# Attention plus FFN on one core: chunk 0 starts on its own rows, shuffled on chip, and the other blocks are prepared inside it

## The reference

```python
qkv = einsum(x, w_qkv); q, k = rope(rmsnorm(q) * q_scale), rope(rmsnorm(k) * k_scale)
out = softmax(q @ k.T * 8 ** -0.5) @ v            # per head, 1024 keys
x = layernorm(x + out @ w_proj + b_proj)
h = silu(x @ w1.T * s1) * (x @ w2.T * s2)         # 128 -> 512
h = gelu(h @ h1.T * sh1); h = gelu(h @ h2.T * sh2)  # 512 -> 512, exact gelu
x = layernorm(x + h @ w3.T * s3)                  # 512 -> 128
```

## Time and profile before

| | us |
|---|---|
| median of 3 runs | 394.11 (391.36 to 394.29) |
| profiled execution: its time | 395.17 |
| its span | 393.5 |
| TensorE busy | 338.4 (86%) |
| ScalarE busy | 306.3 (78%) |
| VectorE busy | 203.4 (52%) |
| GpSimd busy | 18.4 (5%) |

### The profile page before, as it was taken

How to read it: one execution, slowest core, us unless ns; L and a number is a source line. 1 busy time by engine, 2 the same in 40 slices (tenths; PEclk the granted TensorE clock), 3 DMA queues, 4 the chain that set the end, 5 groups by cost and what they waited for, 6 DMA issues and landing times.

```text
span 393.5 us, 6182 instructions
## 1 busy us (share of the span) xinstructions
PE 338.4 (86%) x2077; PEld 136.4 (35%) x2077; DVE 203.4 (52%) x397; ACT 306.3 (78%) x347; POOL 18.4 (5%) x21
## 2 busy tenths in 40 slices
PE   7977287887799998988899989988999899869990
PEld 2533111111133244433322444442223435325760
DVE  1799844311054664455447624554467253556764
ACT  1458289999999988798999889869998987771530
POOL 2400000000010000001100000001100000011001
PEclk9989679999999999999999999989999999898997
DMA  7987953033021230030303300303030200000001
...
DMA packets 16201, 31.33 MB, mean 80 GB/s; under 512 B 1522, under 2 KB 5106, under 8 KB 16178
## 3 DMA queue, kind: packets, MB, share of 16 engines
...
q0 software_dynamic: 240, 0.79, 0.5%
...
## 4 chain that ended last, share of the span: by engine, by line
PE 55%; ACT 20%; DVE 12%; issue 11%; ACTq 0%; DVEq 0%; POOLq 0%; POOL 0%
PE ps L455 17%; ACT probs L714 17%; PE ps L502 14%; PE ps L442 9%; PE ps L576 4%; PE ps L492 4%; DVE ffn L894 2%; DVE probs L801 2%; DVE probs L810 2%; PE ps L628 1%; PE ps L612 1%; PE ps L594 1%; PE ps L415 1%; DVE parts L790 1%; PE ps L472 1%
## 5 line engine op out<-in xcount | busy, mean ns | idle before, releaser
L714 ACT ACTIVATE probs<-ps 128x1024 f32<-128x1024 f32 x256 | 241.3, 1049 | 33.7 <-PE ps L442 33.6
L455 PE MATMUL ps<-probs,va 128*9 128x512 f32 x1024 | 131.0, 601 | 14.1 <-ACT probs L714 12.3
L442 PE MATMUL ps<-qa,ka 32*128 32x512 f32 x512 | 74.3, 501 | 17.8 <-ACT probs L714 11.7
L442 PEld LDWEIGHTS ps<-qa,ka 32*128 32x128 f32 x512 | 29.8, 184 | 115.1 <-ACT probs L714 72.7
L894 DVE TENSOR_SCALAR ffn<-ps,col 128x512 f32<-128x512 f32 x36 | 27.0, 751 | 55.0 <-PE ps L502 50.9
L502 PE MATMUL ps<-g_hi,w_hi 128*128 128x512 f32 x108 | 47.0, 435 | 2.4 <-DVE ffn L894 2.4
L502 PE MATMUL ps<-g_lo,w_hi 128*128 128x512 f32 x108 | 44.1, 409 | 0.0
L455 PEld LDWEIGHTS ps<-probs,va 128*9 128x9 f32 x1024 | 17.8, 89 | 62.6 <-ACT probs L714 32.4
L831 DVE STREAM_TRANSPOSE o_tok<-ps 128x512 f32<-128x512 f32 x15 | 10.7, 715 | 46.0 <-PE ps L455 46.0
L502 PEld LDWEIGHTS ps<-g_hi,w_hi 128*128 128x128 f32 x108 | 21.0, 194 | 15.6 <-DVE ffn L894 4.3
L869 DVE TENSOR_TENSOR g_lo<-ffn,g_hi 128x512 fp32r<-128x512 f32 x36 | 24.9, 692 | 1.2
...
## 6 DMA issues: line engine op xcount, KB each, us to landing
...
va<-v_all SPq DMA_DIRECT2D x16, 144.0 KB, 4.5
...
```

Source lines behind the costliest of these rows:

```text
L442: mm = pe.matmul(s_tile(u)[:, i, :], ka[rows, slot, kt * P:(kt + 1) * P], qa[rows, slot, :], start=True, stop=not shifted)
L455: mm = pe.matmul(ps[32 * h:32 * h + VW, O_BANK, :], va[:, g % 2, kt, h, :], probs[:, step % 4, h, :], start=(kt == 0), stop=(kt == KT - 1))
L714: nc.scalar.activation(probs[:, step % 4, 2 * pair:2 * pair + 2, :], s_tile(u), ACT.Exp).then_inc(exp_done, 1)
```

## The change

- The prologue prepares only what chunk 0's first groups need: k and q of block 0, k of block 1 and V of blocks 0 and 1, each in instructions of 512 columns. Input loads are put on two queues, SP's and ScalarE's.
- Rows of head groups 0 and 1 no longer go through DRAM for chunk 0: `direct_rows` takes them from the prepared tile with a shuffle among 32 partitions, a copy that rounds to the high part, and a scaled sum that writes the rows into `ka` and `qa`. The columns of the weights are permuted on the host so that a group's features lie in each 32 partitions; `strips` reads the DRAM rows in the matching order. V of these groups is read from `v_all`. Groups 2 and 3 and all later chunks still go through DRAM.
- The other q and k (`LATE`: five tiles) and V of blocks 2 and 3 are made inside chunk 0: 18 tasks (`TASKS`) at fixed slots (`TASK_SLOTS`) through bank 7, with squares and inverse roots between ScalarE's exponentials (`SQUARE_STEPS`, `RINV_STEPS`).
- The FFN weights are loaded by GpSimd in three stages into a smaller buffer, and split in pieces among VectorE's late work; the bias is added on VectorE at the end of chunk 0.
- One warm-up of 13 matmuls becomes one of 8; the second, of 10, goes. ScalarE loads the table for the later chunks after chunk 0.
- The form with row maxima (`wide == 1`) is changed to match; it does not run.

```diff
-MIX_FIRST = 1
+MIX_FIRST = 18
...
+WARM = 8
...
+DIRECT = {0: 2, 2: 3, 4: 4, 8: 6, 12: 7}
+LATE = ((1, Q), (2, K), (2, Q), (3, K), (3, Q))
+TASKS = (("proj", 0), ("swap", 0), ("var", 0),
+ ("proj", 1), ("swap", 1), ("var", 1),
+ ("proj", 2), ("swap", 2), ("var", 2), ("v", 2),
+ ("proj", 3), ("swap", 3), ("var", 3),
+ ("proj", 4), ("swap", 4), ("var", 4), ("v", 3), ("flag", 0))
+TASK_SLOTS = (12, 18, 20, 23, 25, 27, 30, 34, 36, 39, 41, 43, 45, 47, 50, 52, 54, 60)
+SQUARE_STEPS = (7, 12, 16, 21, 24)
+RINV_STEPS = (11, 14, 19, 23, 27)
...
+def strips(scr, g):
+    return scr.rearrange("(j r) t -> j r t", j=HG)[:, bass.ds(HD * PARTS * PARTS * g, HD * PARTS * PARTS)]
...
+    sp.dma_start(wq[:, 0:4 * P], w_qkv[:, 0:4 * P]).then_inc(in_w, 16)
+    sp.dma_start(col[:, 0:NCOL], cols).then_inc(in_cols, 16)
+    sp.dma_start(sinT[:, 0:CH], sines[:, 0:CH]).then_inc(in_rope[0], 16)
+    load_x(1)
+    sp.dma_start(wq[:, 4 * P:5 * P], w_qkv[:, 4 * P:5 * P]).then_inc(in_wv, 16)
+    sp.dma_start(sinT[:, CH:SEQ], sines[:, CH:SEQ]).then_inc(in_rope[1], 16)
     for t in range(2, NCH):
-        sp.dma_start(xT[:, t * CH:(t + 1) * CH], x_t[:, t * CH:(t + 1) * CH]).then_inc(in_x[t], 16)
+        load_x(t)
...
+    store(0, 0, 0)
+    store(1, 0, 1)
+    store(2, 1, 0)
...
+        stored_rows((0, 1), (0,))
         load_group(0, 2)
+        store(3, 1, 1)
+        store(4, 2, 0)
         load_group(0, 3)
-        later_loads(False)
+        store(5, 2, 1)
+        store(6, 3, 0)
+        stored_rows((), (1,))
+        load_group(1, 0)
+        store(7, 3, 1)
+        for g in range(1, NG):
+            load_group(1, g)
+        stored_rows((2, 3), (2, 3))
+        sp.wait_ge(v_evac, 4)
...
-    pool.wait_ge(in_res, 64)
-    pool.tensor_tensor(xb[:], xb[:], bias_b[:, None, :].to_broadcast([P, NCH * TILES, P]), ALU.add).then_inc(res_add, 1)
+    def stage(src, at, blocks):
+        pool.dma_start(w_raw[:, at:at + blocks * src.shape[1]].rearrange("p (k o) -> p k o", k=blocks),
+                       src.rearrange("(k p) o -> p k o", p=P)).then_inc(in_ffn, 16)
+    pool.wait_ge(qk_proj, 4)
+    stage(h1, 0, HM)
+    pool.wait_ge(w_taken, 1)
+    stage(h2, 0, HM)
+    pool.wait_ge(w_taken, 2)
+    stage(w1, 0, 1)
+    stage(w2, HID, 1)
+    stage(w3, 2 * HID, HM)
...
+    def first_task(n):
+        kind, i = TASKS[n]
+        bank = mix(0)
+        if n == 0:
+            pe.wait_ge(rot_done, 6)
+        if kind == "flag":
+            pe.wait_ge(w_split, 1)
+            mm = pe.matmul(bank[0:1, 0:1], ve[:, 0:1], ones_c[:], start=True, stop=True)
+        elif kind == "v":
+            mm = project_v(bank, i)
+        elif kind == "var":
+            pe.wait_ge(late_sq, i + 1)
+            mm = variance(bank, late_sets[i % 2][0])
+        else:
+            t, of = LATE[i]
+            pe.wait_ge(in_x[t], 16)
+            mm = proj(of + (QS if kind == "swap" else 0), bank, t)
+        mm.then_inc(mix_ready, 1)
+    def first_chunk(shifted):
+        use[0], given = 0, 0
+        for step in range(STEPS):
+            logits(0, step, 0, shifted)
+            logits(0, step, 1, shifted)
+            if 2 * step in TASK_SLOTS:
+                first_task(TASK_SLOTS.index(2 * step))
+            if step == 1:
+                pe.wait_ge(o_rows_set, 1)
+            if step:
+                values(0, step - 1)
+            if 2 * step + 1 in TASK_SLOTS:
+                first_task(TASK_SLOTS.index(2 * step + 1))
+        assert use[0] == len(TASKS) == MIX_FIRST
...
+    proj(K, ps[:, 0, :], 0).then_inc(qk_proj, 1)
+    proj(KS, ps[:, 1, :], 0).then_inc(qk_proj, 1)
+    pe.wait_ge(in_means, 16)
+    pe.wait_ge(sq_done, 1)
+    variance(ps[:, 4, :], sq_k).then_inc(var_ready, 1)
+    proj(Q, ps[:, 2, :], 0).then_inc(qk_proj, 1)
+    proj(QS, ps[:, 3, :], 0).then_inc(qk_proj, 1)
+    pe.wait_ge(sq_done, 2)
+    variance(ps[:, 5, :], sq_q).then_inc(var_ready, 1)
+    pe.wait_ge(in_x[1], 16)
+    proj(K, ps[:, MIX_BANK, :], 1).then_inc(qk_proj, 1)
+    proj(KS, ps[:, O_BANK, :], 1).then_inc(qk_proj, 1)
+    pe.wait_ge(in_wv, 16)
+    pe.wait_ge(ln_done, 2)
+    project_v(ps[:, 5, :], 0).then_inc(v_proj, 1)
+    pe.wait_ge(sq_done, 3)
+    variance(ps[:, 4, :], sq_k1).then_inc(var_ready, 1)
+    pe.wait_ge(rot_done, 2)
+    project_v(ps[:, 0, :], 1).then_inc(v_proj, 1)
     pe.wait_ge(bound_flag, 1)
     wide = pe.value_load(flags_i[0:1, 0:1], min_val=0, max_val=1)
-    pe.wait_ge(rot_done, 4 * NCH)
-    pe.wait_ge(ln_done, NCH)
-    for _ in range(WARM_AGAIN):
-        pe.matmul(ps[:, 4, :], warm[:, 0:P], warm[:], start=True, stop=True)
-    pe.wait_ge(v_evac, NCH)
-    pe.wait_ge(in_res, 64)
+    pe.wait_ge(rot_done, 4)
+    pe.wait_ge(v_evac, 2)
+    pe.wait_ge(ln_done, 3)
...
+    act.dma_start(xT[:, 0:CH], x_t[:, 0:CH]).then_inc(in_x[0], 16)
+    act.dma_start(cosT[:, 0:CH], cosines[:, 0:CH]).then_inc(in_rope[0], 16)
+    act.dma_start(mean8[:], means).then_inc(in_means, 16)
+    act.dma_start(srow[:], scale_rows).then_inc(in_scales, 16)
+    act.dma_start(cosT[:, CH:SEQ], cosines[:, CH:SEQ]).then_inc(in_rope[1], 16)
...
+    def inverse_root(n, bank, dst):
+        act.wait_ge(var_ready, n)
+        nc.scalar.activation(dst, bank, ACT.Ln, bias=eps_c[:]).then_inc(ln_done, 1)
+        act.wait_ge(ln_done, n)
+        nc.scalar.activation(dst, dst, ACT.Exp, scale=-0.5).then_inc(rinv_done, 1)
...
+    act.wait_ge(qk_proj, 1)
+    square(ps[:, 0, :], sq_k)
+    inverse_root(1, ps[:, 4, :], rinv_k)
+    act.wait_ge(qk_proj, 3)
+    square(ps[:, 2, :], sq_q)
+    inverse_root(2, ps[:, 5, :], rinv_q)
+    act.wait_ge(qk_proj, 5)
+    square(ps[:, MIX_BANK, :], sq_k1)
+    take_v(1, ps[:, 5, :])
+    inverse_root(3, ps[:, 4, :], rinv_k1)
+    take_v(2, ps[:, 0, :])
...
+    def late_square(n):
+        act.wait_ge(mix_ready, TASKS.index(("proj", n)) + 1)
+        if n >= 2:
+            act.wait_ge(parts_done, PARTS * (n + 2))
+        nc.scalar.activation(late_sets[n % 2][0], ps[:, MIX_BANK, :], ACT.Square).then_inc(late_sq, 1)
+    def late_inverse_root(n):
+        at = TASKS.index(("var", n))
+        dst = late_sets[n % 2][0]
+        act.wait_ge(mix_ready, at + 1)
+        nc.scalar.activation(dst, ps[:, MIX_BANK, :], ACT.Ln, bias=eps_c[:]).then_inc(mix_free, 1)
+        act.wait_ge(mix_free, at + 1)
+        nc.scalar.activation(dst, dst, ACT.Exp, scale=-0.5).then_inc(rinv_done, 1)
...
+        if step in SQUARE_STEPS:
+            late_square(SQUARE_STEPS.index(step))
+        if step in RINV_STEPS:
+            late_inverse_root(RINV_STEPS.index(step))
+    act.preload_act_table_set("exp_and_others")
...
+    def turned_by(bank, of, t, dst):
+        table, at = ((cosT, (C_Q, C_K)), (sinT, (C_QS, C_KS)))[of >= QS]
         half = (t % 2) * CH
-        dve.wait_ge(sq_done, t + 1)
-        wait(dve, h_done, t)
-        for i, c_, table, dst in ((0, C_Q, cosT, rot_a), (1, C_K, cosT, rot_a), (2, C_QS, sinT, rot_b), (3, C_KS, sinT, rot_b)):
-            if i == 2:
-                if t:
-                    low_part(t - 1)
-                dve.wait_ge(qk_proj, 2 * t + 2)
-            nc.vector.scalar_tensor_tensor(
-                out=dst[:, (i % 2) * CH:(i % 2 + 1) * CH], in0=ps[:, i, :], scalar=col[:, c_:c_ + 1],
-                in1=table[:, half:half + CH], op0=ALU.mult, op1=ALU.mult).then_inc(rot_done, 1)
-        dve.wait_ge(rot_done, 4 * t + 4)
-        link(nc.vector.tensor_tensor(rot_a, rot_a, rot_b, ALU.add), 0)
-        if t == NCH - 1:
-            dve.wait_ge(v_evac, t)
-            nc.vector.memset(ps[:, O_BANK, :], 0.0).then_inc(o_rows_set, 1)
-        dve.wait_ge(rinv_done, t + 1)
-        nc.vector.tensor_tensor(hn, rot_a, rinv, ALU.mult).then_inc(h_done, 1)
-    dve.wait_ge(h_done, NCH)
-    last = parts_of(NCH - 1)
-    nc.vector.tensor_copy(last[:, 0, :], hn).then_inc(last_parts, 1)
-    dve.wait_ge(last_parts, 1)
-    nc.vector.tensor_tensor(last[:, 1, :], hn, last[:, 0, :].bitcast(F32), ALU.subtract).then_inc(last_parts, 1)
+        return nc.vector.scalar_tensor_tensor(out=dst, in0=bank, scalar=col[:, at[of % 2]:at[of % 2] + 1],
+                                              in1=table[:, half:half + CH], op0=ALU.mult, op1=ALU.mult)
+    def rope_of(count, h, rot, rinv, n):
+        dve.wait_ge(rot_done, count)
+        link(nc.vector.tensor_tensor(h, h, rot, ALU.add), 0)
+        dve.wait_ge(rinv_done, n)
+        link(nc.vector.tensor_tensor(h, h, rinv, ALU.mult), 0)
...
+    def direct_rows(h, lo, n, g, low, dst):
+        src = spread[:, 0:n]
+        wait(dve, direct, written[0])
+        written[0] += 1
+        link(nc.vector.stream_shuffle(src, h[:, lo:lo + n], [HD * g + m // 4 for m in range(32)]), 0)
+        link(nc.vector.tensor_copy(x_hi[:, 0:n], src), 0)
+        nc.vector.scalar_tensor_tensor(out=dst, in0=x_hi[:, 0:n].bitcast(F32), scalar=col[:, low:low + 1], in1=src,
+                                       op0=ALU.mult, op1=ALU.add).then_inc(direct, 1)
...
+    def rows_parts(n, t, at, h):
+        if t >= 2:
```

(157 more changed lines are left out.)

309 lines of the change are left out of this document (132 added, 177 removed).

## The result

Measured side by side, the kernel after takes 411.88 us (409.33 to 414.11, 4 runs) against 394.12 (391.36 to 394.29): ratio 1.0468, 95% interval 1.0424 to 1.0513. The change makes the kernel slower by 17.8 us. The forecast was 404.6, 390 to 411: right in direction, 7.3 us too low, and 0.9 us outside its range.

What follows compares the result with a forecast made beforehand. The prologue and ScalarE's exponentials in chunk 0 were taken to bound the kernel. Prologue -24.0, chunk 0 +33.9 and boundary +0.6 gave +10.5 us: 405.7 against the profiled execution, 404.6 against the median, range 390 to 411.

Steps and rivals of the forecast that it cites:

- first exponential: End of the prologue: ScalarE's first exponential of chunk 0 comes at 23.4 us instead of 47.36, a gain of 24.0.
- ScalarE's own work in chunk 0: Chunk 0: 58.9 us of exponentials plus 9.0 of squares, logarithms, small exponentials and hand-over, 67.9 us.
- entry of chunk 0 at low clock: Start of chunk 0: TensorE, slow after its gap, adds 1.1 us, as before the change.
- S: Chunk 0: stalls since all 18 tasks share one bank and ScalarE and TensorE are strictly in order, 20.1 us.
- F: Chunk 0: falls of TensorE's clock after idle gaps, three taken at 4.8 us, bounds 0 and six falls, 9.6.
- boundary: Before chunk 1: ScalarE's table load of 1.28 us, beside the 0.69 it waits there now, adds 0.6 us.
- steps 13 and 22: Chunk 0: two swap tasks in the same step as the square releasing their bank's reader, 2.45 us idle each.
- six falls in chunk 0 alone: Chunk 0: rival with six clock falls, 409 us; chance 0.15 together with VectorE being late.
- The fetch: Before the first logits: TensorE's jump over the unused form of chunk 0 stalls for instructions again, 6.1 us.
- Hidden hand-overs: Chunk 0: rival with next logits already in PSUM when ScalarE comes back, net -10.4, 383.7 us; chance 0.13.
- the border S + F = 14.4: Chunk 0: stalls plus clock falls below 14.4 us make the change faster, with the fetch counted.
- VectorE's lateness: Chunk 0: rival with late rows of group 1 or late V, 3 to 5 us more; chance 0.15 with more falls.

Runs made afterwards that it cites:

- a_fill: The kernel after, with 3 to 10 matmuls on zeros on TensorE before ten of the 18 tasks, while it would wait: 404.38 us, ratio 1.0238.
- the two exchanges: TensorE's form for wide == 0 put before the one for wide == 1: in the kernel after 407.61 us, in the kernel before 386.92 us.
- a_resched: The kernel after, with squares, inverse roots and tasks at other steps and VectorE's list in matching order, same work: 384.04 us, ratio 0.973.

## Why the direction was right and the size was not

The change point by point, all in the profiled executions, where the forecast was 405.7 and the time 409.33: 3.6 us off.

| | forecast | after | off |
|---|---|---|---|
| first exponential | 23.4 | 22.34 | -1.1 |
| ScalarE's own work in chunk 0 | 67.9 | 69.5 | +1.6 |
| entry of chunk 0 at low clock | 1.1 | 1.5 | +0.4 |
| stalls and falls, S + F | 20.1 + 4.8 | 25.9 | +1.0 |
| chunk 0 | 93.9 | 96.9 | +3.0 |
| boundary | +0.6 | +0.6 | 0 |
| later chunks and tail | 0 | +1.7 | +1.7 |

Chunk 0 is 22.34 to 119.24; 25.9 is the 32.1 us of waits less 4.7 before the first exponential and 1.5 at steps 2 and 3 (0.97 + 0.56); the own work is what is left.

**The stalls were right one by one.** `a_fill` gives them at full clock. Its 26.3 us of waits less 4.5 at the start and 1.5 at steps 2 and 3 (1.10 + 0.42) are 20.3; the forecast's S was 20.1. By place, forecast and `a_fill`: steps 13 and 22, 2.45 and 2.50 each; steps 18 and 26, 1.6 and 1.72; step 28, 2.0 and 2.00; steps 12, 20 and 24, 1.0 and 0.98 to 1.02; step 10, 1.7 and 2.00; step 21, 1.7 and 1.46. Chains built from single rows of before (read, product, wake, projection, logits) hold to 0.1 us where no VectorE queue is in them.

**The mis-sized term is the clock, F.** It was set to three falls in chunk 0, 4.8 us, and to none elsewhere. The profiled execution had four falls behind the entry, 25.9 - 20.3 = 5.6. The forecast counted them by the length of TensorE's gaps, and the length does not decide alone. Of TensorE's nine idle stretches over 1.3 us in chunk 0 of after, behind its entry, those of 1.38, 2.39, 2.39 and 1.79 us had a fall behind them, and three of 1.63, one of 1.78 and the longest, 2.61, had none. TensorE's lines behind the shortest of the nine (the clock is 0.50 from 44 to 46 us) and the longest (1.00 from 109 to 113):

```profile
42.69 1.78 PE L447 MATMUL ps<-xT,wq 128*128 128x512 f32 x2 [1.38 <-DVE ffn L899]
...
109.20 1.16 PE L451 MATMUL ps<-wq,xT 128*128 128x128 f32 x8 [2.61 <-ACT ffn L812]
```

The profiled execution also had a longer fall in chunk 1, and this lies outside the forecast's sum: ScalarE waits 4.38 us at the place where before waited 1.33, and one less of 1.6 in chunk 2 (1.33 where before had 2.94). That makes +1.4 of the +1.7. ScalarE's timeline of after, chunks 1 and 2:

```profile
196.99 3.77 ACT L822 ACTIVATE probs<-ps 128x1024 f32<-128x1024 f32 x4 [4.38 <-PE ps L478]
...
276.93 3.77 ACT L822 ACTIVATE probs<-ps 128x1024 f32<-128x1024 f32 x4 [1.33 <-PE ps L478]
```

The other 3.6 us are the medians': the profiled execution of after is the fastest of its four, 2.5 below the median, and that of before 1.1 above its own. The forecast knew the second and could not know the first. So the profiled execution alone would lie inside the range of 390 to 411, and the median misses it by 0.9. Executions of after differ in how long TensorE is at low clock: the mean granted clock is 0.946, 0.943, 0.942 and 0.939 for 409.33, 411.66, 412.09 and 414.11 us. With the idle stretches filled the spread falls to 0.5 us at 0.965 to 0.967. So a change that leaves TensorE waiting at many places pays for the falls and for their chance as well, and the range's upper end, six falls in chunk 0 alone, was too near. That the kernel with fills is 7.5 us faster is shown, although its profiled prologue was 1.95 us slower. So at the medians the falls may cost 9 us and not 4.8, an estimate that takes all its executions to have had that slow prologue. How the chance of a fall divides over the places is not shown.

**ScalarE's own work** was short by 1.6. One exponential alone takes 1.02 us, two in a row 1.94, four 3.77: 0.92 each, and 0.1 more at the end of the row. The sum had 0.92 for all, and after breaks the row 18 times with a wait, which by this estimate is 1.8 us.

**The fetch.** Mechanism right, size not: 6.1 was taken, and 3.9 were seen, 2.2 less. Against that the V copies ended 1.0 later than worked out (17.62, not 16.6) and the step from logits to exponential took 0.2 more, so the forecast start is only 1.1 too late, and luck hides half of the error. Where the form stands first the gap is gone in both kernels. The queue's line for 16 to 22 us of after shows one 16 KB transfer, where the gap of before has two:

```profile
q8 instruction: 1, 0.02, 1.3%
```

The DMA queues moved 351 GB/s in the gap of before (40.4 to 46.4 us) and 4 in that of after (17.6 to 21.6). Whether the number of transfers or this traffic makes the gap of before longer is open. The Trainium skill ("Runtime: NRT & Kernel Launch", section "Instruction fetch mechanics") says that a taken branch to a target that is not held waits until its page is fetched. The transfers in both gaps and the two exchanges agree with it; a size for it only the runs give.

**The rivals.** Hidden hand-overs were priced at 383.7 with S about 4 and F 0. The change doesn't do this, but `a_resched` does, at 384.04 with 3.8 us of waits behind the first exponential: the border S + F = 14.4 was the right thing to watch, and one order of the same work lies on each side of it. That the two times are so close is in part luck: S is 2.5 and not 4 (without steps 2 and 3) and the start is 1.1 sooner, but ScalarE's own work is 1.1 longer. That the clock, not VectorE's lateness, would be what adds to the stalls was given too little chance.
